# Layer 1 one-hot tables with token columns innermost, and constant bf16 ramps

## The chip, the cores and the metric

One core of a Trainium2 chip runs the whole program. The metric is the device time of one execution in microseconds (us), the median of a few runs.

## The reference, cut to what matters

Sixteen images and texts pass through a tokenizer, a selective-scan layer and a mixture of experts (layer 0), then through causal attention and a second mixture of experts (layer 1). Only the routing of the second mixture is touched:

```
logits = xf @ wr + br                      # tokens x 4 experts
topk_vals, topk_idx = top_k(logits, 2)     # each token has two experts
gates = softmax(topk_vals)
out = sum over the two of gates * (y_expert - c_expert + c_sum)
```

The 16 * 165 tokens are held as 22 tiles of up to 128 rows (16 text tiles, 6 image tiles), so there are 44 (choice, tile) columns.

## The kernel before, in words

**Tables of places.** The kernel sorts the (token, choice) pairs by expert into 48 slots (`SLOT1`) of 128 places. `positions` (line 571), on VectorE, works out for each pair its place; `high7` is the slot, `low7` the row in it. To invert that map it builds one-hot tables in bf16 and lets TensorE multiply them (lines 613 to 625):

- `intile1[p, i, 2, s]` is 1 where pair column i of token row p lies in slot s (line 616, 44 x 48 elements); `intile1[.., 0, ..]` is that times the tile number (line 619), `intile1[.., 1, ..]` that times the token row (line 621).
- `inrow1[p, i, r]` is 1 where the pair's row is r (line 624, in two halves of 22 columns i, 22 x 128 elements each).

The compares take one fp32 operand with the pair's number repeated along the inner dimension, and one fp32 constant (`k_slot`, `k_iota`) that runs along it; the product of line 619 reads the fp32 constant `k_tile`. So the innermost dimension is the slot (48) or the row (128), and each table is dense along it.

`pe_slots` (line 526) then runs 44 matmuls on TensorE into one PSUM bank: for column i the stationary operand is `inrow[:, i, :]` (128 dense columns) and the moving operand is `intile[:, i, :, :]` (3 x 48 = 144 dense columns). It waits for the first half of `inrow1` before column 0 and for the second before column 22. The matmul in the trace stands at line L531. The sum in PSUM holds, for each place, the tile, the row and whether it is taken; VectorE turns it into the lists `source` and `dest` (lines 637 to 645) by which GpSimd gathers and scatters rows.

**Order around it.** Engines run their instructions in the order written. On TensorE `pe_layer1` (line 1624) issues `biases_out(2)`, `pe_count`, `biases_sum` (line 1639: 96 matmuls at L1648 and 4 fp32 ones, recorded as 8, at L1651), the slot matmuls, and then the expert matmuls. On VectorE `positions` is followed by the last bias term (line 1703), two absolute maxima over weights (L658), the scale of the activations, and the experts. Layer 0 uses the same `positions` with one choice, 22 columns and 24 slots.

**Start of attention.** Layer 0's last expert output is scattered by GpSimd (L871) onto rows in DRAM; SyncE waits for that and loads the sums back as the residual `h`. ScalarE (`act_attention`, line 1321) meanwhile copies prepared weights (lines 1359 to 1363) and then takes the square roots for the first norm (`roots`, line 1364; the activation is at L1814). VectorE (`dve_attention`, line 1435) zeroes three small tiles, splits a bias (lines 1507 and 1508), waits for the last output product of layer 0 (`y_done`, line 1509) and for the first residual tiles (line 1510), and takes their statistics (L1439).

The buffer `X` holds layer 0's weights first, then the working tiles of attention (`rx`), then those of layer 1's experts (`rg`) in the same words. `early` holds the one-hot tables.

Of the kernel before, what the change touches and what calls it, by code (L numbers as in the profile page):

```python
# [8 lines left out]
BF16 = mybir.dt.bfloat16  # L9
# [3 lines left out]
ALU = mybir.AluOpType  # L13
ACT = mybir.ActivationFunctionType
# [3 lines left out]
P = 128  # L18
# [13 lines left out]
NT = BATCH + IT  # L32
# [7 lines left out]
SLOT0 = (BATCH * SEQ + G0 * (P - 1)) // P  # L40
W0N = 2 * KC * F0 + (F0 // P) * D

E1, F1, TOPK = 4, 1024, 2
T1 = 2 * P
PAIRS1 = (TOPK * BATCH * SEQ + E1 * (T1 - 1)) // T1
SLOT1 = 2 * PAIRS1
# [99 lines left out]
def known(i, value):  # L146

    return isinstance(i, int) and i == value
# [18 lines left out]
def build(nc, txt, patches, wtok, cols, rows_a, consts, pe_table, wsmall, w0, wattn, rows_f, w1, wsmall1,  # L167
          b2rows, out):
    with ExitStack() as ctx:
        def sb(name, shape, dt=F32):  # L170
            return ctx.enter_context(nc.sbuf_tensor(name, shape, dt))

        def sem(name):
            return ctx.enter_context(nc.semaphore(name))
# [4 lines left out]
        X = sb("X", [P, XW])  # L179
# [28 lines left out]
        low7 = rc[:, 0:TOPK, :].bitcast(I32)  # L208
        high7 = rc[:, TOPK:2 * TOPK, :].bitcast(I32)
# [3 lines left out]
        PS = ctx.enter_context(nc.psum_tensor("PS", [P, 8, 512], F32))  # L213
# [14 lines left out]
        k_slot = cst[:, at:at + SLOT1]; at += SLOT1  # L228
        k_far = cst[:, at:at + NT]; at += NT
        k_tile = cst[:, at:at + TOPK * NT]; at += TOPK * NT  # L230
        k_iota = cst[:, at:at + P]; at += P
        k_row, k_patch, k_class = (cst[:, at + i:at + i + 1] for i in range(3))
# [70 lines left out]
        XE = XW - W1W // 2 - 2 * E1 * D  # L303
# [4 lines left out]
        rx = Region(X, XE)  # L308
# [12 lines left out]
        oTi = rx.take([KC, PB * IMG])  # L321
        nmax, smax, psum_, rsum = (rx.take([2]) for _ in range(4))

        rg = Region(X, XE)
        early = Region(X, XE, rg.at)
        inrow1, intile1 = early.take([TOPK * NT, P], BF16), early.take([TOPK * NT, 3, SLOT1], BF16)
        hh1 = rg.take([2, 4, T1])
        wall1 = rg.take([SLOT1])
        bias1 = rg.take([2, F1 // P])
# [91 lines left out]
        y_done = sem("y_done")  # L421
        y_copied = sem("y_copied")
        y_out = [sem("y_out0"), sem("y_out1")]
        hot_ready = sem("hot_ready")
        map_psum = sem("map_psum")
# [92 lines left out]
        def pe_count(pe, done):  # L518
# [4 lines left out]
            nc.tensor.matmul(PS[:, 7, 128:128 + 4 * NT], onesb[:, :], flat, start=True, stop=True)\  # L523
                .then_inc(count_psum, 1)

        def pe_slots(pe, done, n, tiles, inrow, intile):

            for i in range(n):
                if i % (n // 2) == 0:
                    pe.wait_ge(hot_ready, 2 * done + i // (n // 2) + 1)  # L530
                ins = nc.tensor.matmul(PS[:, 7, 0:3 * tiles], inrow[:, i, :], intile[:, i, :, :].rearrange("p a b -> p (a b)"),  # L531
                                       start=(i == 0), stop=(i == n - 1))
            ins.then_inc(map_psum, 1)
# [30 lines left out]
        def dest_of_token(dve, chain, tiles, from_, to, taken):  # L564
# [3 lines left out]
            chain.link(nc.vector.tensor_tensor(to, spare[:, 0:tiles], to, ALU.subtract))  # L568
            chain.link(nc.vector.tensor_tensor(to, to, from_, ALU.add))

        def positions(dve, chain, choices, tiles, done, inrow, intile, unit):


# [9 lines left out]
            flat = lambda ap: ap.rearrange("p g t -> p (g t)")  # L583
# [17 lines left out]
            for c in range(choices):  # L601
# [4 lines left out]
            slots_of = posf[:, 0:choices, :]  # L606
# [3 lines left out]
            chain.link(nc.vector.tensor_scalar(high7[:, 0:choices, :], pos[:, 0:choices, :], 7, None,  # L610
                                               ALU.logical_shift_right))
            n = choices * NT
            chain.link(nc.vector.tensor_copy(slots_of, high7[:, 0:choices, :]))
            each = lambda ap, m: ap.rearrange("p c t -> p (c t)").unsqueeze(2).broadcast_to([P, n, m])
            along = lambda ap, m: ap.unsqueeze(1).broadcast_to([P, n, m])
            chain.link(nc.vector.tensor_tensor(intile[:, :, 2, :], each(slots_of, tiles), along(k_slot[:, 0:tiles], tiles),
                                               ALU.is_equal))
            chain.link(nc.vector.tensor_copy(slots_of, low7[:, 0:choices, :]))
            nc.vector.tensor_tensor(intile[:, :, 0, :], intile[:, :, 2, :],
                                    k_tile[:, 0:n].unsqueeze(2).broadcast_to([P, n, tiles]), ALU.mult)  # L620
            nc.vector.tensor_scalar(intile[:, :, 1, :], intile[:, :, 2, :], k_row, None, ALU.mult)
            half = n // 2
            for c0 in (0, half):
                nc.vector.tensor_tensor(inrow[:, c0:c0 + half, :], each(slots_of, P)[:, c0:c0 + half],
                                        along(k_iota, P)[:, c0:c0 + half], ALU.is_equal).then_inc(hot_ready, 1)

            units = tiles // unit
            sf = tok[:, 0, 0:units]
# [692 lines left out]
        def act_attention(act, roots):  # L1321
            act.wait_ge(small1_loaded, 16)
            nc.scalar.activation(gb1, c_b1c, ACT.Gelu).then_inc(gb_ready, 1)

            def image(n):
                act.wait_ge(xi_tr, n + 1)
                nc.scalar.activation(xTi[:, :, n * IROWS:(n + 1) * IROWS],
                                     PS[:, IMAGE_BANK[n], 0:KC * P].rearrange("p (k r) -> p k r", k=KC)[:, :, 0:IROWS],
                                     ACT.Copy).then_inc(xTi_copied, 1)

            def text(b, slot):
                act.wait_ge(xn_tr, AHEAD + NF + b + 1)
                nc.scalar.activation(xTb[:, slot, :, IMG:SEQ], PS[:, 7, 0:KC * P].rearrange("p (k r) -> p k r", k=KC),
                                     ACT.Copy).then_inc(xTb_copied, 1)

            def exps(b):
                act.wait_ge(s_max, b + 1)
                nc.scalar.activation(pA, sA1, ACT.Exp, bias=nmax[:, 0:1], scale=SCALE, accum_out=psum_[:, 0:1])
                nc.scalar.activation(pB[0:SEQ - P, :], sB1[0:SEQ - P, :], ACT.Exp, bias=nmax[0:SEQ - P, 1:2], scale=SCALE,
                                     accum_out=psum_[0:SEQ - P, 1:2]).then_inc(p_exp, 1)  # L1340

            def copy_pt(b):
                act.wait_ge(pt_psum, b + 1)
                nc.scalar.activation(pT1, PS[:, 4, 0:SEQ], ACT.Copy)
                nc.scalar.activation(pT2[0:SEQ - P, :], PS[0:SEQ - P, 4, SEQ:2 * SEQ - P], ACT.Copy).then_inc(pt_copied, 1)

            def copy_ot(b):
                act.wait_ge(ot_psum, b + 1)
                o_ = PS[:, 5, 0:KC * SEQ].rearrange("p (k r) -> p k r", k=KC)
                nc.scalar.activation(oTb, o_[:, :, IMG:SEQ], ACT.Copy).then_inc(ot_copied, 1)  # L1350
                nc.scalar.activation(oTi[:, :, bass.ds(b * IMG, IMG)], o_[:, :, 0:IMG], ACT.Copy).then_inc(ot_copied, 1)

            def chunk(n, k, j):

                act.wait_ge(stage_full[k], 16 * (j + 1))
                nc.scalar.activation(w1h[:, bass.ds(n * CW, CW)], stage[:, k, :], ACT.Copy).then_inc(w_high, 1)

            act.wait_ge(prep_psum, 3)
            nc.scalar.activation(wfT.rearrange("p k n -> p (k n)"), PS[:, 3, 0:KC * D], ACT.Copy)
            nc.scalar.activation(bfT, PS[:, 5, 0:KC], ACT.Copy).then_inc(prep_copied, 1)  # L1360
            act.wait_ge(prep_psum, 4)
            nc.scalar.activation(wfx[:, :, D:PAY1], PS[:, 5, 8:8 + KC * E1].rearrange("p (k e) -> p k e", k=KC), ACT.Copy)
            nc.scalar.activation(sums1, PS[:, 5, 8 + KC * E1:8 + (KC + 2) * E1], ACT.Copy).then_inc(prep_copied, 1)
            roots(0, BATCH + 1)
            image(0)
            text(0, 0)
            text(1, 1)
            roots(BATCH + 1, IT - 1)
            for n in range(1, IT):
                image(n)  # L1370


            def run(b, slot, j):
                exps(b)
                copy_pt(b)
                if known(b, 1):
                    roots(4, BATCH - 4)
                if not (isinstance(b, int) and b >= BATCH - 2):
                    text(b + 2, slot)
                copy_ot(b)  # L1380
                chunk(b, slot, j)
            run(0, 0, 0)
            run(1, 1, 0)
            with act.Fori(1, BATCH // 2 - 1) as j:
                run(2 * j, 0, j)
                run(2 * j + 1, 1, j)
            run(BATCH - 2, 0, BATCH // 2 - 1)
            run(BATCH - 1, 1, BATCH // 2 - 1)
# [46 lines left out]
        def dve_attention(dve, chain, inverse_roots):  # L1435
# [67 lines left out]
            chain.link(nc.vector.memset(smax[:, :], 0.0))  # L1503
            chain.link(nc.vector.memset(psum_[:, :], 1.0))
            chain.link(nc.vector.memset(raw1, 0.0))
            dve.wait_ge(gb_ready, 1)
            chain.link(nc.vector.tensor_copy(gbh, gb1))
            nc.vector.tensor_tensor(gbl, gb1, gbh, ALU.subtract).then_inc(gb_split, 1)
# [67 lines left out]
            for t in range(BATCH):  # L1576
                ins = nc.vector.bn_aggr(mv[:, t, :], stats[:, t, 0, :])
# [46 lines left out]
        def pe_layer1(pe):  # L1624
# [32 lines left out]
            biases_out(2)  # L1657
            pe_count(pe, 1)
            biases_sum()
            pe_slots(pe, 1, TOPK * NT, SLOT1, inrow1, intile1)  # L1660
            pe.wait_ge(slots_ready, 2)
            pe.wait_ge(dest_ready, 2)
            pe.wait_ge(rest_ready, 1)
# [775 lines left out]
```

## Time and profile before

| what | value |
|---|---|
| runs | 890.33 us median of 3 (890.0 to 891.31) |
| the profiled execution, its own time | 891.11 us |
| its span, first to last instruction | 889.3 us |
| granted TensorE clock, mean share of full speed | 0.935 |
| TensorE matmul busy | 776.2 us (87%), 5506 instructions |
| VectorE busy | 521.9 us (59%) |
| ScalarE busy | 366.0 us (41%) |
| GpSimd busy | 366.2 us (41%) |
| chain that ended last: TensorE, VectorE, GpSimd | 75%, 12%, 5% |

The profiled execution lies 0.78 us above the median. Its time is its span and 1.8 us around it. In the rows further down PE is TensorE's matmul, PEld its weight load, DVE VectorE, ACT ScalarE, POOL GpSimd, SPq the queue of SyncE; L531 is line 531 of the kernel, which can be that of a helper. A clock of 1.00 is TensorE's 2.4 GHz, 0.50 is 1.2 GHz.

### The profile page before, as it was taken

How to read it: one execution, taken by the hardware profiler on the slowest of the kernel's cores; microseconds unless marked ns; L12 is line 12 of the kernel's file. 1: busy time of each engine (PE TensorE's matmuls, PEld its weight loads, DVE VectorE, ACT ScalarE, POOL GpSimd, SP SyncE). 2: the span in 40 equal slices, each digit the busy share in tenths (PEclk: the TensorE clock that was granted, in tenths of full speed). 3: DMA queues.
4: the chain of work that ended last, by engine and by line, in shares of the span. 5: the costliest groups of instructions: out<-in, count | busy, mean ns of one | idle time of the engine just before them, and what ended most of it. 6: DMA issues, size and time to landing. Idle time of an engine off the chain costs nothing.

```text
span 889.3 us, 17678 instructions
## 1 busy us (share of the span) xinstructions
PE 776.2 (87%) x5506; PEld 609.1 (68%) x5507; DVE 521.9 (59%) x1300; ACT 366.0 (41%) x795; POOL 366.2 (41%) x314
## 2 busy tenths in 40 slices
PE   3898904999999999478999998958999999999991
PEld 2677802666666666356777776747898999999981
DVE  5898888433333333286777877884555555555550
ACT  5795671333333333224343343503444444444430
POOL 3349931223232322134455552012555555555442
PEclk9998965999999999878999997977999999999996
DMA  9950132232121111331111211521233332232325
GB/s 259 417 200 1 66 123 91 68 76 30 30 30 30 30 30 25 95 118 46 50 47 51 67 47 47 182 76 38 43 51 51 48 48 48 48 48 48 42 25 145
DMA packets 37042, 66.98 MB, mean 75 GB/s; under 512 B 3552, under 2 KB 29264, under 8 KB 35312
## 3 DMA queue, kind: packets, MB, share of 16 engines
q1 hardware_dynamic: 22992, 47.16, 15.9%
q0 software_dynamic: 13824, 19.01, 13.7%
q8 instruction: 19, 0.31, 0.2%
q10 hardware_dynamic: 192, 0.38, 0.1%
q14 instruction: 15, 0.12, 0.0%
HBM read 45.49 MB, written 23.74 MB: 78 GB/s over the span
## 4 chain that ended last, share of the span: by engine, by line
PE 75%; DVE 12%; POOL 5%; ACT 2%; DMA 2%; issue 1%; SPq 0%; POOLq 0%; DVEq 0%; ACTq 0%
PE PS L899 14%; PE PS L707 14%; PE PS L912 14%; PE PS L725 7%; PE PS L1208 5%; POOL X L1794 4%; PE PS L1218 3%; PE PS L1227 2%; PE PS L715 2%; PE PS L1256 2%; PE PS L1246 1%; PE PS L885 1%; DMA Y<-in_wtok_dram 1%; PE PS L1248 1%; PE PS L1969 1%
## 5 line engine op out<-in xcount | busy, mean ns | idle before, releaser
L1051 POOL DMA_INDIRECT sum<-X,dest x48 | 97.4, 2029 | 107.4 <-ACT X L966 95.3
L707 PE MATMUL PS<-X,Y 128*128 x576 | 134.3, 384 | 1.3 <-DVE Y L805 1.3
L912 PE MATMUL PS<-X 128*128 x768 | 133.5, 273 | 1.8 <-ACT X L966 1.8
L899 PE MATMUL PS<-X 128*128 128x256 f16 x768 | 130.2, 275 | 1.5 <-DVE X L984 1.5
L956 ACT ACTIVATE X<-PS,X 128x256 f32<-128x256 f32 x192 | 75.3, 475 | 109.9 <-PE PS L899 109.9
L899 PE MATMUL PS<-X,Y 128*128 128x256 f16 x384 | 105.5, 275 | 0.0
L912 PE MATMUL PS<-Y,X 128*128 x384 | 104.7, 273 | 0.0
L816 DVE SCALAR_TENSOR_TENSOR Y<-PS,Y 128x512 f32<-128x512 f32 x48 | 36.1, 751 | 111.5 <-PE PS L707 111.5
L871 POOL DMA_INDIRECT sum<-Y,dest x24 | 38.1, 1586 | 148.0 <-ACT Y L782 148.0
L707 PEld LDWEIGHTS PS<-X,Y 128*128 128x128 f16 x576 | 56.9, 99 | 60.8 <-issue 4.3
L899 PEld LDWEIGHTS PS<-X 128*128 x768 | 75.6, 99 | 11.4 <-issue 2.1
L912 PEld LDWEIGHTS PS<-X 128*128 128x128 f16 x768 | 75.1, 98 | 10.5 <-issue 2.1
L1038 POOL DMA_INDIRECT X<-xs,source x48 | 47.3, 985 | 70.5 <-DVE source L642 41.8
L725 PE MATMUL PS<-X,Y 128*128 x576 | 70.8, 273 | 2.4 <-DVE Y L822 1.7
L1011 DVE SCALAR_TENSOR_TENSOR PS<-PS,hscale,X 128x256 f32<-128x256 f32 x48 | 21.2, 488 | 79.1 <-PE PS L912 79.1
L1003 DVE SCALAR_TENSOR_TENSOR X<-X,hscale 128x1024 f16<-128x1024 f32 x48 | 61.6, 1284 | 1.7
L725 PEld LDWEIGHTS PS<-X,Y 128*128 128x128 f16 x576 | 56.1, 98 | 9.1 <-issue 3.1
L1794 POOL TENSOR_TENSOR X<-X 128x256 f16<-128x256 f32 (+1 forms) x55 | 58.2, 1097 | 0.5
L775 ACT ACTIVATE Y<-PS,hscale 128x512 f16<-128x512 f32 x48 | 33.0, 688 | 55.7 <-PE PS L715 55.7
L769 ACT ACTIVATE Y<-PS 128x512 f32<-128x512 f32 x48 | 28.7, 597 | 62.9 <-PE PS L707 62.9
L1405 POOL TENSOR_TENSOR X<-X 128x330 f32<-128x330 f32 x32 | 28.4, 886 | 62.7 <-DVE X L1467 62.7
L1208 PE MATMUL PS<-X,Y 128*128 128x165 f32 x256 | 47.0, 329 | 0.0
(356 smaller groups left out, 1499.1 us busy)
## 6 DMA issues: line engine op xcount, KB each, us to landing
X<-in_w_dram SPq DMA_DIRECT2D x11, 1024.0 KB, 17.4
stage<-in_w_dram SPq DMA_DIRECT2D x16, 512.0 KB, 3.5
sum<-h SPq DMA_DIRECT2D x2, 2048.0 KB, 7.5
xs<-Y SPq DMA_DIRECT2D x2, 1040.0 KB, 5.0
xs<-Y SPq DMA_DIRECT2D x2, 1032.0 KB, 5.5
h<-in_txt_dram SPq DMA_DIRECT2D x2, 1024.0 KB, 18.3
Y<-in_patches_dram SPq DMA_DIRECT2D x3, 672.0 KB, 8.8
sum<-h SPq DMA_DIRECT2D x2, 768.0 KB, 3.9
```

Source lines behind the costliest of these rows:

```text
L707: ins = nc.tensor.matmul(PS[:, 2 * u + s, 0:F0], x_[:, slot, k, :], w_[:, at_:at_ + F0], start=(n == 0), stop=(n == 3 * KC - 1))
L725: ins = nc.tensor.matmul(PS[:, 6, 0:D], h_[:, s, c, :], w_[:, at_:at_ + D], start=(s == 0 and c == 0 and n == 0), stop=(s == 1 and c == 3 ...
L816: nc.vector.scalar_tensor_tensor(out=hh[:, s, :].unsqueeze(1), in0=PS[:, 2 + s, 0:F0].unsqueeze(1), scalar=wall[:, bass.ds(i, 1), s], in1= ...
L871: nc.gpsimd.indirect_dma_start(out=sum0, out_offset=bass.IndirectOffsetOnAxis(ap=dest[:, i:i + 1], axis=0), in_=ybuf[:, i % 2, :], in_offs ...
L899: ins = nc.tensor.matmul(PS[:, 2 * s + c // 2, (c % 2) * T1:(c % 2 + 1) * T1], part[:, off:off + P], x_[:, slot, k, :], start=(n == 0), st ...
L912: ins = nc.tensor.matmul(PS[:, 4 + a, 0:D], h_[:, s, c, a * P:(a + 1) * P], part[:, off:off + D], start=(s == 0 and c == 0 and n == 0), st ...
L956: ins = nc.scalar.activation(hh1[:, s, c, :], PS[:, 2 * s + c // 2, (c % 2) * T1:(c % 2 + 1) * T1], ACT.Gelu, bias=bias1[:, slot, f:f + 1])
L1003: nc.vector.scalar_tensor_tensor(out=lo_, in0=act_, scalar=hscale[:, 2:3], in1=hi_, op0=ALU.mult, op1=ALU.subtract).then_inc(h1_lo, 1)
L1038: nc.gpsimd.indirect_dma_start(out=x1in[:, n // 2 % 2, n % 2, :], out_offset=None, in_=xs1, in_offset=bass.IndirectOffsetOnAxis(ap=source[ ...
L1051: nc.gpsimd.indirect_dma_start(out=sum1, out_offset=bass.IndirectOffsetOnAxis(ap=dest[:, i:i + 1], axis=0), in_=y1buf[:, i // 2 % 2, i % 2 ...
L1208: ins = nc.tensor.matmul(PS[:, bank, m * SEQ:(m + 1) * SEQ], w_[:, k, m * P:(m + 1) * P], xTb[:, slot, k, :], start=(k == 0), stop=(k == K ...
L1794: ins = nc.gpsimd.tensor_tensor(w0_low(n)[:, of], w0_landing(n)[:, of], w0_high(n)[:, of], ALU.subtract)
```

## The change

The tables of layer 1 are turned round: `inrow1` becomes [row, column] and `intile1` [kind, slot, column], with the 44 columns innermost. The operand that ran along the inner dimension becomes a filled table in bf16: `ramp_row` (128 x 44) and `ramp_tile` (44) are written by ScalarE ahead of `roots`, `ramp_slot` (48 x 44) by VectorE after a wait for `y_done`. They take 3,938 words of `X` behind attention's tiles. The pair's numbers are copied to bf16 (`lowb`, `highb`) and repeated along the middle dimension. TensorE now reads both operands with a step of 44 elements. Layer 0 keeps its form, in a function of its own (`one_hots0`).

```diff
@@ regions
+        ramp_row, ramp_slot = rx.take([P, TOPK * NT], BF16), rx.take([SLOT1, TOPK * NT], BF16)
+        ramp_tile = rx.take([TOPK * NT], BF16)
+        lowb, highb = rx.take([TOPK * NT], BF16), rx.take([TOPK * NT], BF16)
...
-        inrow1, intile1 = early.take([TOPK * NT, P], BF16), early.take([TOPK * NT, 3, SLOT1], BF16)
+        inrow1, intile1 = early.take([P, TOPK * NT], BF16), early.take([3, SLOT1, TOPK * NT], BF16)
@@ TensorE
+        def pe_slots1(pe):
+
+            n = TOPK * NT
+            for i in range(n):
+                if i % NT == 0:
+                    pe.wait_ge(hot_ready, 2 + i // NT + 1)
+                ins = nc.tensor.matmul(PS[:, 7, 0:3 * SLOT1], inrow1[:, :, i],
+                                       intile1[:, :, :, i].rearrange("p a b -> p (a b)"), start=(i == 0), stop=(i == n - 1))
+            ins.then_inc(map_psum, 1)
@@ VectorE, for layer 1 in place of lines 613 to 625
+        def one_hots1(chain):
+
+            n = TOPK * NT
+            each = lambda ap, m, k: ap.unsqueeze(1).broadcast_to([P, m, k])
+            flat = lambda ap: ap.rearrange("p c t -> p (c t)")
+            nc.vector.tensor_copy(highb, flat(high7))
+            chain.link(nc.vector.tensor_copy(lowb, flat(low7)))
+            chain.link(nc.vector.tensor_tensor(intile1[:, 2], each(highb, SLOT1, n), ramp_slot, ALU.is_equal))
+            nc.vector.tensor_tensor(intile1[:, 0], intile1[:, 2], each(ramp_tile, SLOT1, n), ALU.mult)
+            nc.vector.tensor_scalar(intile1[:, 1], intile1[:, 2], k_row, None, ALU.mult)
+            for c0 in (0, NT):
+                of = slice(c0, c0 + NT)
+                nc.vector.tensor_tensor(inrow1[:, :, of], each(lowb[:, of], P, NT), ramp_row[:, :, of], ALU.is_equal)\
+                    .then_inc(hot_ready, 1)
@@ ScalarE, in act_attention ahead of roots(0, BATCH + 1)
+            spread = lambda ap, n: ap.unsqueeze(2).broadcast_to([P, n, TOPK * NT])
+            nc.scalar.activation(ramp_row, spread(k_iota, P), ACT.Copy)
+            nc.scalar.activation(ramp_tile, k_tile, ACT.Copy)
@@ VectorE, in dve_attention behind the memsets (ahead of line 1506)
+            dve.wait_ge(y_done, SLOT0)
+            nc.vector.tensor_copy(ramp_slot, k_slot.unsqueeze(2).broadcast_to([P, SLOT1, TOPK * NT]))
@@ pe_layer1
-            pe_slots(pe, 1, TOPK * NT, SLOT1, inrow1, intile1)
+            pe_slots1(pe)
```

## Rows read from the trace of the kernel before

**Rows 1.** The page: the chain that ended last, by line.

```profile
PE PS L899 14%; PE PS L707 14%; PE PS L912 14%; PE PS L725 7%; PE PS L1208 5%; POOL X L1794 4%; PE PS L1218 3%; PE PS L1227 2%; PE PS L715 2%; PE PS L1256 2%; PE PS L1246 1%; PE PS L885 1%; DMA Y<-in_wtok_dram 1%; PE PS L1248 1%; PE PS L1969 1%
```

**Rows 2.** The chain in order of time, 578 to 606 us: start us, us, what.

```profile
578.98 2.37 DVE X L616
...
584.63 6.01 DVE X L624 x2
...
590.69 2.83 PE PS L531 x22
...
593.55 0.22 DVE stats L637
...
602.03 0.77 PE PS L683 x2
```

**Rows 3.** VectorE's groups with shapes kept apart: mean ns after the busy time.

```profile
L624 DVE TENSOR_TENSOR X<-posf,cst 128x2816 bf16<-128x2816 f32 x2 | 6.1, 3084 | 0.0
...
L624 DVE TENSOR_TENSOR Y<-posf,cst 128x1408 bf16<-128x1408 f32 x2 | 3.2, 1618 | 0.0
...
L619 DVE TENSOR_TENSOR X<-X,cst 128x2112 bf16<-128x2112 bf16 x1 | 2.4, 2357 | 0.0
...
L621 DVE TENSOR_SCALAR X<-X,cst 128x2112 bf16<-128x2112 bf16 x1 | 0.8, 762 | 0.0
```

**Rows 4.** TensorE's timeline around 584 to 591 us.

```profile
583.92 1.99 PE L1651 MATMUL PS<-X,onesf 1*128 1x256 f32 x8
587.69 1.94 PE L531 MATMUL PS<-X 128*128 128x144 bf16 x22 [1.78 <-DVE X L624]
```

**Rows 5.** TensorE's slot matmuls and weight loads, line L531.

```profile
L531 PEld LDWEIGHTS PS<-X x44: 95/151/152, 587.7 to 593.1; 128*128 128x128 bf16 x44
L531 PE MATMUL PS<-X x44: 226/327/328, 587.7 to 593.2; 128*128 128x144 bf16 x44
```

**Rows 6.** Short stretches around the slot matmuls: PE, PEld, DVE, ACT, POOL, clock, DMA.

```profile
587.60:588.20 0.60, 0.51 (x8) 0.51 (x9) 0.60 (x2) 0.00 (x0) 0.00 (x0) 1.00 0.00 0
...
588.80:589.40 0.60, 0.60 (x8) 0.54 (x5) 0.60 (x1) 0.00 (x0) 0.00 (x0) 0.50 0.00 0
```

**Rows 7.** VectorE's reductions, by shape (L553 reads at a step of 22 words).

```profile
L1484 DVE TENSOR_REDUCE X<-X 128x1 f32<-128x128 f32 x16 | 4.6, 286 | 0.6
...
L553 DVE TENSOR_REDUCE ra<-ra 128x22 f32<-128x88 f32 x2 | 0.6, 301 | 0.1
...
L593 DVE TENSOR_REDUCE sm<-ra 128x4 f32<-128x44 f32 x1 | 0.2, 199 | 0.0
```

**Rows 8.** ScalarE's timeline before attention, and its later square root.

```profile
371.04 1.28 ACT L1814 ACT_TABLE_LOAD   x1
378.45 0.22 ACT L1814 ACTIVATE rs<-rs 128x17 f32<-128x17 f32 x1 [6.13 <-DVE rs L2140]
```

**Rows 9.** ScalarE's copies and exponentials by shape.

```profile
L1356 ACT ACTIVATE X<-stage 128x1024 f16<-128x1024 f32 x4 | 4.2, 1058 | 0.0
...
L1338 ACT ACTIVATE X<-X 128x128 f32<-128x128 f32 x16 | 6.4, 402 | 29.9 <-DVE X L1485 29.9
```

**Rows 10.** VectorE's timeline while the residual is awaited.

```profile
368.11 0.18 DVE L1507 CAST wsm<-wsm 128x32 f16<-128x32 f32 x1 [3.50 <-ACT wsm L1323]
...
376.00 1.73 DVE L1439 BATCH_NORM_STATS2 stats<-h 128x6 f32<-128x256 f32 x5 [7.47 <-DMA h<-sum]
```

**Rows 11.** The chain in order of time, 355 to 382 us.

```profile
364.39 1.58 PE PS L725 x12
...
366.75 3.82 DMA sum<-Y,dest
```

**Rows 12.** GpSimd's scatters: line L871, and one of L1051 in the timeline.

```profile
L871 POOL DMA_INDIRECT sum<-Y,dest x24: 1552/1587/1624, 166.0 to 366.7; - x24
...
648.01 2.34 POOL L1051 DMA_INDIRECT sum<-X,dest  x1 [3.83 <-ACT X L966]
```

**Rows 13.** VectorE's timeline beside that scatter.

```profile
647.60 1.28 DVE L1003 SCALAR_TENSOR_TENSOR X<-X,hscale 128x1024 f16<-128x1024 f32 x1
```

More of the change, by code:

```diff
@@ L322, in build @@
         nmax, smax, psum_, rsum = (rx.take([2]) for _ in range(4))
-        rg = Region(X, XE)
-        early = Region(X, XE, rg.at)
-        inrow1, intile1 = early.take([TOPK * NT, P], BF16), early.take([TOPK * NT, 3, SLOT1], BF16)
+        ramp_row, ramp_slot = rx.take([P, TOPK * NT], BF16), rx.take([SLOT1, TOPK * NT], BF16)
+        ramp_tile = rx.take([TOPK * NT], BF16)
+        lowb, highb = rx.take([TOPK * NT], BF16), rx.take([TOPK * NT], BF16)
+        ramps_at = rx.at - TOPK * NT * (P + SLOT1 + 3) // 2
+        rg = Region(X, ramps_at)
+        early = Region(X, ramps_at, rg.at)
+        inrow1, intile1 = early.take([P, TOPK * NT], BF16), early.take([3, SLOT1, TOPK * NT], BF16)
         hh1 = rg.take([2, 4, T1])
@@ L569, in dest_of_token, with one_hots0 @@
             chain.link(nc.vector.tensor_tensor(to, to, from_, ALU.add))
+        def one_hots0(chain, slots_of, inrow, intile):
+            chain.link(nc.vector.tensor_copy(slots_of, high7[:, 0:1, :]))
+            each = lambda ap, m: ap.rearrange("p c t -> p (c t)").unsqueeze(2).broadcast_to([P, NT, m])
+            along = lambda ap, m: ap.unsqueeze(1).broadcast_to([P, NT, m])
+            chain.link(nc.vector.tensor_tensor(intile[:, :, 2, :], each(slots_of, SLOT0), along(k_slot[:, 0:SLOT0], SLOT0),
+                                               ALU.is_equal))
+            chain.link(nc.vector.tensor_copy(slots_of, low7[:, 0:1, :]))
+            nc.vector.tensor_tensor(intile[:, :, 0, :], intile[:, :, 2, :],
+                                    k_tile[:, 0:NT].unsqueeze(2).broadcast_to([P, NT, SLOT0]), ALU.mult)
+            nc.vector.tensor_scalar(intile[:, :, 1, :], intile[:, :, 2, :], k_row, None, ALU.mult)
+            half = NT // 2
+            for c0 in (0, half):
+                nc.vector.tensor_tensor(inrow[:, c0:c0 + half, :], each(slots_of, P)[:, c0:c0 + half],
+                                        along(k_iota, P)[:, c0:c0 + half], ALU.is_equal).then_inc(hot_ready, 1)
+        def one_hots1(chain):
[11 more added lines that the diff above has]
+                    .then_inc(hot_ready, 1)
         def positions(dve, chain, choices, tiles, done, inrow, intile, unit):
@@ L612, in positions @@
             n = choices * NT
[L613 to L625, printed above, removed]
+            if choices == 1:
+                one_hots0(chain, slots_of, inrow, intile)
+            else:
+                one_hots1(chain)
             units = tiles // unit
```

## The prediction

> **What bounds the kernel now.** The page is read first: the chain that ended last belongs mostly to TensorE's expert products, and no line of this change is in its list [rows 1]. So the share of busy time says nothing here; the chain in order of time does. From 578.98 us it runs through VectorE's one-hot tables of layer 1 (L616 to L624, until 590.64 us), then through the last 22 slot matmuls until 593.52 us, and at 593.55 us VectorE reads the result [rows 2]. Behind that come small chained steps, two maxima over weights and, at 602.03 us, TensorE's first work for the experts [rows 2]. Between the slot matmuls and that point VectorE is never without work and TensorE has none, so whatever moves 593.52 us moves the end by as much. The reader should see two candidates for that point: VectorE's tables, and TensorE, whose timeline shows it busy with the bias sums until 585.91 us and idle for only 1.78 us before the first slot matmul [rows 4].
>
> **The tables on VectorE.** Five large instructions are replaced by five with the same numbers of elements. Now each two-source one takes one element per cycle or so: 1,408 elements take 1,618 ns, 2,816 take 3,084 and 2,112 take 2,357 [rows 3]. No row shows a two-source instruction whose operands are all 2-byte. Its bounds are no gain (2,357 and 3,084 ns) and the rate of the one-source instruction that is all bf16, 2,112 elements in 762 ns [rows 3]. I take the middle, two elements per cycle: a half of `inrow1` then costs what 1,408 elements cost now, 1.62 us, and a table of 2,112 some 1.26 us (the fixed part is 2 * 1,618 - 3,084 = 152 ns, the rest halves). The scalar product stays at 0.76 us, its rate being reached already. The two small copies stand where two stood. Counted from 578.98 us, allowing 0.1 us for the copy that now comes earlier: 579.1, plus 1.26, 1.2 and 0.7, then 1.55 for a half (successive ones overlap a little). The first half is ready at about 583.9 us in place of 587.69, the second at 585.4 in place of 590.64. That is 5.2 us of VectorE time gone.
>
> **What is late next.** TensorE does the bias sums first, in program order, and their last fp32 products could be followed at 585.75 us at the earliest: 1.99 us for 8, each lasting 0.387 us, gives a pitch of 0.23 us, and the next one starts a pitch after the eighth [rows 4]. So the faster tables are worth 1.94 us at the first half, and from there all 44 matmuls run without a wait. Their end is 585.75 us + 43 pitches + 0.35 us of the last one's own time and its semaphore. It was 593.52 us, so the break-even pitch is 173 ns.
>
> **The pitch of a slot matmul.** Now it is 8 starts in 0.51 us, 63 ns, while the clock is 1.00, and at 0.50 it is (2.83 - 0.327) / 21 = 119 ns [rows 2, 5, 6]: 144 columns at one per cycle of 2.4 or 1.2 GHz. The weight loads take 95 to 152 ns and run beside the matmuls [rows 5]. Afterwards every column of both operands is 88 bytes from the last. No row shows TensorE reading so. The lower bound is no cost, 63 ns. The nearest row for the other end is VectorE's reduction at L553, which reads fp32 at this very step of 22 words: contiguous reductions take 286 ns for 128 elements and 199 ns for 44, so 1.036 ns each and 153 ns fixed, which makes 245 ns for 88; L553 takes 301 [rows 7]. That is 0.64 ns more per element, 1.68 ns in all. If this is the time in which the memory gives one element of a distant line, it holds for TensorE too whatever its clock, and 144 columns take 242 ns. I take 242 ns, since it is the only row with this step; the end is then 585.75 + 43 * 0.242 + 0.35 = 596.5 us, which is 3.0 us late.
>
> The page "SBUF — State Buffer" of the Trainium skill (section Door 1, its note on cachelines) speaks against this change: the memory has lines of 16 bytes, at least two accesses must fall in one to hide its latency, and 8 bf16 elements is as far as a step goes free. The row of L553 agrees in kind. The page gives no price for TensorE; without the rule the sum would be that of the first rival below. "VectorE: DVE Perf Modes" (The perf-mode tier table) gives two elements per cycle for an all-bf16 two-source instruction; no row here shows it.
>
> **The ramps on ScalarE.** One copy of 5,632 elements and one of 44. A copy of 1,024 takes 1,058 ns and an exponential of 128 takes 402 [rows 9], so 0.73 ns per element and 4.5 us at the least, 5.8 us if everything scales with 1,058; with the small one 4.7 to 6.0 us. The queue is free when the table load of 1.28 us begins, at 371.04 us; the load then comes behind the copies, and the square root is wanted at 378.45 us [rows 8]: it would be ready between 377.0 and 378.3 us. The cover is the wait for the residual; it costs nothing, with 0.15 us left at the slow end. Behind these copies stand only the roots, for which VectorE waits.
>
> **The ramp on VectorE.** 2,112 elements, between 0.76 [rows 3] and 2.36 us. VectorE is idle until 368.11 us and again from 368.5 to 376.00 us [rows 10], and its wait for `y_done` ends with layer 0's last product at 365.97 us [rows 11], so itself it delays only the bias split, which TensorE first uses for layer 1's bias sums, after the whole of attention. But it lies beside GpSimd's last scatter, issued at 366.75 us, which is on the chain too [rows 11]. The scatters of layer 0 take 1,587 ns; one that begins at 648.01 us, beside VectorE's two-input product until 648.88 us, takes 2,340 [rows 12, 13]. So 0.87 us side by side costs 0.75 us. A copy at two elements per cycle would run from 366.05 to 367.35 us, 0.6 us beside the scatter: plus 0.5 us. Bounds: nothing, and 1.4 us for a copy of 2.36 us.
>
> **Sum.** 3.0 + 0.5 = 3.5 us. The sum is against the profiled execution (891.11 us, so 894.6 us); against the median of the runs, 0.78 us lower, it is 890.33 + 3.5 = **893.8 us**. No DMA is added or moved, and SyncE's queue is passed by nothing. A measurement of this kernel can tell about 0.2%, 1.8 us, from no change.
>
> **The rivals.**
> - Distant columns are free for TensorE. It starts warm at 585.75 us, straight behind the bias sums, and the clock, which fell to 0.50 here after the 1.78 us gap [rows 4, 6], need not fall. 585.75 + 43 * 0.063 + 0.25 = 588.7 us, 4.8 us early; with the scatter 4.3: 886.0 us. This is the other side; it decides below 173 ns of pitch. For it: no row shows TensorE itself losing anything to a step. Against: L553. Chance 0.24.
> - Half speed, 120 ns: 585.75 + 5.16 + 0.3 = 591.2 us, 2.3 early, with the scatter 1.8 us: 888.5 us, at the edge of what can be told. For it: a penalty in cycles of the reader's own clock (L553 loses 0.6 of a cycle per element). Chance 0.19, and 0.05 for pitches around the break-even.
> - The weight loads, 128 distant columns, 215 ns by the same row, no longer run beside the matmuls: pitch 457 ns, end 605.8 us, 12.2 late: 903 us. Against it: they overlap now [rows 5]. Chance 0.05.
> - The change doesn't do what it says: the all-bf16 compares stay at one element per cycle. The first half is then ready at 587.7 us as now, and with 242 ns the end is 598.5 us: 5.5 us in all, 895.8 us (0.04); with plain pitches, nothing moves (0.01).
> - Likeliest, 893.8 us: 0.42.
>
> **The numbers.** Slower: 0.42 + 0.05 + 0.04 = 0.51. The half-speed case is split, 0.12 to no change and 0.07 to faster; with 0.05 and 0.01 no change has 0.18. Faster: 0.24 + 0.07 = 0.31. Cases of both signs hold much of the chance, so the range reaches from 885.6 (columns free, a scatter undisturbed) to 896.5 us (the compares at one per cycle, the scatter at its bound) and leaves out the serial weight loads and tails. The likeliest case's own range is 892.3 to 895.6 us.
>
> **What would show it.** Right: bf16 tables of 1.26 and 1.62 us; slot matmuls from 585.8 us on in one run of 44 without a gap, at a pitch near 0.24 us; a longer last scatter at L871 in attention's start, and the first statistics about 0.5 us later; the square root still waiting for VectorE. Wrong: a pitch of 63 or 120 ns, or a clock that falls amid them and changes the pitch, which would say that it is counted in TensorE's cycles and not in the memory's time.

## The result, and the profile after

The changed kernel takes 897.29 us (median of 6), the kernel before 890.82 us in the same comparison: a ratio of 1.0076, interval 1.0055 to 1.0097, so 4.9 to 8.6 us slower. One of the six runs of the kernel before took 4,457.89 us; it moves the median little, and the ratio is taken from the undisturbed runs. The forecast said slower, 893.8 us, and the range ended at 896.5 us. The sign and most of the steps held; one term was sized too small.

The chain of the changed kernel in order of time, 575 to 608 us (start us, us, what), beside [rows 2]:

```profile
574.99 7.64 PE PS L1690 x70
582.63 1.92 PE PS L1693 x8
584.55 14.81 PE PS L537 x44
...
599.39 0.22 DVE stats L674
...
602.66 4.40 DVE tops L695 x2
...
607.86 0.77 PE PS L720 x2
```

VectorE's tables are no longer in it. TensorE's bias sums (L1690, L1693) are followed at once by all 44 slot matmuls (L537), which take 14.81 us. The stretch from the first copy of the pair's numbers to VectorE's read of the result lasts from 577.39 to 599.39 us, 22.0 us; before it was 14.79 us (578.76, the copy just ahead of L616's 578.98, to 593.55 [rows 2]). That is 7.2 us lost in one place. The profiled span grew by only 5.5 us (894.8 against 889.3), because this execution was already 1.5 us ahead at layer 0's first scatter (164.5 against 166.0 us [rows 12]), where nothing is changed. Behind VectorE's read the two run alike: 295.4 us to the end, against 295.7 before.

VectorE's timeline of the changed kernel, 575 to 600 us:

```profile
577.39 0.19 DVE L607 CAST X<-rc 128x44 bf16<-128x44 int32 x1
...
577.70 1.26 DVE L609 TENSOR_TENSOR X<-X 128x2112 bf16<-128x2112 bf16 x1
579.00 1.26 DVE L610 TENSOR_TENSOR X<-X 128x2112 bf16<-128x2112 bf16 x1
580.17 0.76 DVE L611 TENSOR_SCALAR X<-X,cst 128x2112 bf16<-128x2112 bf16 x1
580.85 3.15 DVE L614 TENSOR_TENSOR X<-X 128x2816 bf16<-128x2816 bf16 x2
...
599.39 0.21 DVE L674 COPY stats<-PS 128x48 f32<-128x48 f32 x1 [14.46 <-PE PS L537]
```

The tables cost 1.26, 1.26, 0.76 and 3.15 us, as against 2.37, 2.36, 0.76 and 6.1 us [rows 2, 3]. Then VectorE waits 14.46 us for TensorE. The reader should see the trade: 5 us less on one engine, some 10 us more on the one behind it (its 44 matmuls took 1.94 and 2.83 us before [rows 2, 4]).

Line L537 of the changed kernel (duration ns min/median/max), beside [rows 5]:

```profile
L537 PEld LDWEIGHTS PS<-X x44: 153/156/177, 584.5 to 598.5; 128*128 128x128 bf16 x44
L537 PE MATMUL PS<-X x44: 523/524/529, 584.5 to 598.8; 128*128 128x144 bf16 x44
```

And short stretches of it. Each line has its length and the busy time of TensorE, its weight load, VectorE, ScalarE and GpSimd, then the granted clock (1.00 or 0.50 here) and, last, two figures on DMA:

```profile
584.50:586.00 1.50, 1.50 (x6) 0.83 (x6) 0.39 (x2) 0.39 (x1) 0.00 (x0) 1.00 0.00 0
...
588.00:590.00 2.00, 2.00 (x8) 0.93 (x6) 0.00 (x0) 0.00 (x0) 0.00 (x0) 0.50 0.00 0
```

A matmul starts every 333 ns, at 1.00 as at 0.50: 44 of them in 14.81 us, and those that start before the clock falls at 587.3 us have the same pitch as those behind.

ScalarE and GpSimd at the start of attention (timeline of ScalarE; then the scatter's line):

```profile
369.22 4.90 ACT L1402 ACTIVATE X<-cst 128x5632 bf16<-128x5632 f32 x1
...
374.25 1.28 ACT L1856 ACT_TABLE_LOAD   x1
377.01 0.22 ACT L1856 ACTIVATE rs<-rs 128x17 f32<-128x17 f32 x1 [1.48 <-DVE rs L2182]
```

```profile
L908 POOL DMA_INDIRECT sum<-Y,dest x24: 1552/1588/2006, 164.5 to 365.2; - x24
```

The ramps cost ScalarE 5.1 us and are hidden with 1.48 us to spare. The last scatter, beside VectorE's copy into `ramp_slot`, takes 2.01 us in place of 1.55. Little of that arrives further on. From this scatter's start to landing it is 4.21 us against 3.82, but the load of the residual behind it took 4.62 us against 4.91, so the first statistics follow the scatter's start by 9.35 us (365.20 to 374.55), against 9.25 before (366.75 to 376.00).

### The profile page after: what moved, and what is told of

The parts are those of the page before. It is cut to its first block, busy times and chain, and to the rows that moved or that the text cites. A ratio compares the mean times of both kernels' runs of the same rounds, so it can differ in the third digit from the quotient of the medians.

```text
span 894.8 us, 17681 instructions
## 1 busy us (share of the span) xinstructions
PE 785.3 (88%) x5506; PEld 611.2 (68%) x5507; DVE 517.2 (58%) x1301; ACT 370.5 (41%) x797; POOL 365.5 (41%) x314
## 4 chain that ended last, share of the span: by engine, by line
PE 78%; DVE 10%; POOL 5%; ACT 2%; DMA 2%; issue 1%; SPq 0%; POOLq 0%; DVEq 0%; ACTq 0%
PE PS L936 14%; PE PS L744 14%; PE PS L949 14%; PE PS L762 7%; PE PS L1245 5%; POOL X L1836 4%; PE PS L1255 3%; PE PS L1264 2%; PE PS L752 2%; PE PS L1293 2%; PE PS L537 2%; PE PS L1283 1%; PE PS L922 1%; PE PS L1285 1%; DMA Y<-in_wtok_dram 1%
```

## The experiments

What stayed open was what 333 ns is made of. Theory A: the moving operand's distant columns alone, 2.3 ns each. Theory B: the two operands' readings one after the other, 156 ns for the stationary one (the weight load's time above) and the rest, 178 ns, for the moving one. In what follows an operand is called turned when it is read with a step of 44 elements, and dense when its columns are adjacent.

**Probes between the tables and the slot matmuls.** The changed kernel with extra matmuls into an unused PSUM bank; their results are not used.

```diff
+        def pe_probes(pe):
+            pe.wait_ge(hot_ready, 4)
+            row_ = ramp_row.rearrange("p a b -> p (a b)")
+            turned = lambda i: intile1[:, :, :, i].rearrange("p a b -> p (a b)")
+            mm = lambda to_, left, right: nc.tensor.matmul(to_, left, right, start=True, stop=True)
+            for i in range(16):
+                mm(PS[:, 3, 0:144], onesb[:, :], turned(i))
+            for i in range(16):
+                mm(PS[:, 3, 0:144], inrow1[:, :, i], row_[:, 0:144])
+            for i in range(16):
+                mm(PS[:, 3, 0:144], onesb[:, :], row_[:, 0:144])
+            for i in range(16):
+                mm(PS[:, 3, 0:48], inrow1[:, :, i], turned(i)[:, 0:48])
...
```

> The turned kernel with 256 extra matmuls between the tables and the slot matmuls (16 groups of 16, one source line each, results unused), dense and with column steps of 2 to 44 elements, on the moving or the stationary side. Theory A: the pitch of 334 ns is the moving operand's reading alone, 144 distant columns at 2.3 ns each. Then a dense stationary with the turned moving operand has 334 ns, and a turned stationary with a dense moving operand stays near 63 to 156 ns. Theory B: the two operands' readings don't run beside each other, 156 ns for the stationary and 178 ns for the moving columns. Then each alone has about 156 to 180 ns. Both: steps of 2 and 4 elements (4 and 8 bytes) cost nothing, 63 ns warm; from 8 elements (16 bytes) on the pitch is that of 44. With 48 turned moving columns A gives about 110 ns or the load's 156, B about 215 ns.

TensorE's timeline of this kernel (the groups share one line, so they are told apart by time and by the tiles that they read; `onesb` is the dense stationary operand):

```profile
585.14 5.49 PE L535 MATMUL PS<-X,onesb 128*128 128x144 bf16 x16
590.44 2.11 PE L535 MATMUL PS<-X 128*128 128x144 bf16 x16
592.35 2.12 PE L535 MATMUL PS<-X,onesb 128*128 128x144 bf16 x16
...
619.46 6.50 PE L535 MATMUL PS<-X 128*128 128x144 bf16 x80
```

and its clock around the last three of them:

```profile
590.50:592.30 1.80, 1.80 (x17) 1.80 (x16) 0.00 (x0) 0.00 (x0) 0.00 (x0) 0.50 0.00 0
592.40:594.20 1.80, 1.80 (x18) 1.80 (x16) 0.00 (x0) 0.00 (x0) 0.00 (x0) 0.50 0.00 0
...
622.00:625.00 3.00, 3.00 (x49) 3.00 (x48) 0.00 (x0) 0.00 (x0) 0.00 (x0) 0.99 0.02 5
```

Dense stationary with turned moving operand: 5.30 us from group to group, 331 ns each. Turned stationary with dense moving operand: 1.91 us, 119 ns, and the group with both dense that follows has the same at the same clock of 0.50. The last 80 have a dense moving operand and stationary steps of 2, 4, 8, 16 and 32 elements: 120 ns each up to 622 us, at 0.50, and at a clock of 0.99 some 47 of them start in 3.0 us, 64 ns each. Theory A holds: the moving side pays it all, and what the stationary side does stays hidden beside it. With only 48 turned moving columns the pitch is 113 ns, where A had expected about 110 or the load's 156, and B 215. The time of this kernel is 938.3 us, the probes included.

In one point both theories were wrong: a step of 4 was to be free and one of 8 or more was to cost what 44 does. Six groups with a dense stationary operand follow, with moving steps of 2, 4, 8, 16, 32 and 1 elements; the windows lie in the groups of 8 and of 32:

```profile
601.40 18.26 PE L535 MATMUL PS<-X,onesb 128*128 128x144 bf16 x96
...
605.40:608.30 2.90, 2.90 (x14) 1.37 (x12) 0.00 (x0) 0.00 (x0) 0.00 (x0) 1.00 0.00 0
...
613.70:617.50 3.80, 3.80 (x17) 1.95 (x16) 0.00 (x0) 0.00 (x0) 0.00 (x0) 0.50 0.00 0
```

From start to start the groups of 8, 16 and 32 have 256, 261 and 244 ns, not 333; at 0.50 the group of 4 has 130 ns, where the group of 2 has 119 and dense ones 120. So the price of a step had to be measured by itself (below).

**One operand turned at a time, in the kernel itself.** `moving_only` keeps `inrow1` dense, `stationary_only` keeps `intile1` dense.

```diff
# moving_only
-        inrow1, intile1 = early.take([P, TOPK * NT], BF16), ...
+        inrow1, intile1 = early.take([TOPK * NT, P], BF16), ...
-                nc.vector.tensor_tensor(inrow1[:, :, of], each(lowb[:, of], P, NT), ramp_row[:, :, of], ALU.is_equal)\
+                nc.vector.tensor_tensor(inrow1[:, of], lowb[:, of].unsqueeze(2).broadcast_to([P, NT, P]),
+                                        k_iota.unsqueeze(1).broadcast_to([P, NT, P]), ALU.is_equal)\
...
# stationary_only
-early.take([3, SLOT1, TOPK * NT], BF16)
+early.take([TOPK * NT, 3, SLOT1], BF16)
...
```

> As the turned kernel, but inrow1 stays dense (its compare at one element per cycle, 3.08 us a half) and only the moving operand intile1 is turned. Theory A: the slot matmuls keep their pitch of 334 ns, and their end is the turned kernel's plus about 1.5 us at most for the later first half. Theory B: the pitch falls to about 178 ns, and the slots end some 5 us earlier than in the turned kernel.

> Only inrow1 is turned (a step of 44 on the stationary side), intile1 stays dense with its compare and product at one element per cycle (2.36 us each). Theory A, that only the moving side pays for its step: the slot matmuls run at 63 to 65 ns when warm and end some 4 us earlier than in the kernel before: about 886 us. Theory B, that the sides add up: a pitch of 220 ns or more, and about 893 us.

The chain of `moving_only`, then that of `stationary_only`:

```profile
583.27 1.92 PE PS L1694 x8
585.19 14.77 PE PS L537 x44
```

```profile
581.41 2.36 DVE X L612
583.77 0.68 DVE X L613
584.45 1.55 DVE X L616
586.04 3.25 PE PS L537 x44
589.31 0.22 DVE stats L676
```

With only the moving operand turned the 44 matmuls take 14.77 us, all of the loss (897.31 us in one run). With only the stationary one turned they take 3.25 us (its weight loads take 151 ns each, beside the matmuls), the kernel's stretch is 10.6 us (578.70 to 589.31) in place of 14.8, and it is faster than the kernel before: 885.69 against 890.49 us, ratio 0.9959, interval 0.9936 to 0.9981. So half of the change was a gain of about 4 us, and the other half lost it and 7 us more.

**The size of the step.** `pad48` pads the table rows to 48 columns; `probes2` puts 23 groups of 10 dense-stationary matmuls with moving steps of 1 to 64 elements ahead of the slots, results unused.

```diff
# pad48
+        inrow1, intile1 = early.take([P, 48], BF16), early.take([3, SLOT1, 48], BF16)
+        inrow1, intile1 = inrow1[:, :, 0:TOPK * NT], intile1[:, :, :, 0:TOPK * NT]
# probes2, one group, here a step of 4
+            for i in range(10):
+                nc.tensor.matmul(PS[:, 3, 0:144], onesb[:, :], flat16[:, 0:576:4], start=True, stop=True)
```

> The turned kernel with its table rows padded from 44 to 48 columns, so a step of 96 bytes in place of 88. Theory L: a column costs 1.7 to 1.8 ns where its step is a multiple of the 16-byte line and 2.3 ns where it is not. Then the pitch falls from 333 to about 250 ns, and the slots end 3.6 us earlier. Theory D: the cost grows with the distance. Then the pitch is 333 ns or more.

> The turned kernel with 23 groups of 10 extra matmuls ahead of the slots, a dense stationary operand, and 144 moving columns with steps of 1 to 8, 12, 16, 20, 22, 24, 28, 32, 36, 40, 44, 46, 48, 52 and 64 elements of 2 bytes, results unused. Theory L: about 250 ns at 8, 16, 24, 32, 40, 48 and 64; about 333 ns at 12, 20, 22, 28, 36, 44, 46 and 52. Theory D: a rise with the step. Both: 1 and 2 at 63 or 119 ns by the clock, 4 at 130 ns.

Padding made it worse. Its chain has

```profile
588.20 15.97 PE PS L538 x44
```

that is a pitch of 360 ns, from the first start at 588.13 to the last at 603.60 us (902.4 us in one run). The groups of `probes2` (953.4 us in one run, the extra matmuls included) have a line each; steps of 1, 2, 3, 4 and 8 elements, then 32, 36, 40, 44, 48, 52 and 64 (the groups left out are in the tables below):

```profile
587.89 0.80 PE L535 MATMUL PS<-X,onesb 128*128 128x144 bf16 x10
588.53 0.80 PE L537 MATMUL PS<-X,onesb 128*128 128x144 bf16 x10
589.17 1.14 PE L539 MATMUL PS<-X,onesb 128*128 128x144 bf16 x10
590.15 1.46 PE L541 MATMUL PS<-X,onesb 128*128 128x144 bf16 x10
...
597.22 2.74 PE L549 MATMUL PS<-X,onesb 128*128 128x144 bf16 x10
...
615.03 2.62 PE L563 MATMUL PS<-X,onesb 128*128 128x144 bf16 x10
617.47 2.91 PE L565 MATMUL PS<-X,onesb 128*128 128x144 bf16 x10
620.20 3.18 PE L567 MATMUL PS<-X,onesb 128*128 128x144 bf16 x10
623.20 3.52 PE L569 MATMUL PS<-X,onesb 128*128 128x144 bf16 x10
...
629.99 3.79 PE L573 MATMUL PS<-X,onesb 128*128 128x144 bf16 x10
633.59 2.93 PE L575 MATMUL PS<-X,onesb 128*128 128x144 bf16 x10
636.34 2.62 PE L577 MATMUL PS<-X,onesb 128*128 128x144 bf16 x10
```

From the start of one group to that of the next, through ten matmuls, the pitch is as follows. The granted clock was 1.00 up to the step of 6, fell within the group of 7, and was 0.50 from 8 on:

| step, elements of 2 bytes | 1 | 2 | 3 | 4 | 5 | 6 | 7 | 8 |
|---|---|---|---|---|---|---|---|---|
| ns for 144 columns | 64 | 64 | 98 | 128 | 161 | 193 | 225 | 256 |

| step | 12 | 16 | 20 | 22 | 24 | 28 | 32 | 36 | 40 | 44 | 46 | 48 | 52 | 64 |
|---|---|---|---|---|---|---|---|---|---|---|---|---|---|---|
| ns | 253 | 261 | 256 | 255 | 252 | 248 | 244 | 273 | 300 | 332 | 347 | 360 | 275 | 244 |

Both theories on the step fall. L (multiples of the line against others) gave 12, 20, 22 and 28 the high price, and they have the low one; 48 was to be low and is the highest. D (a rise with the distance) is right only up to 8 and from 32 to 48. Three regions are shown: from 4 to 16 bytes the pitch is 32 ns times the step; from 16 to 64 bytes it is flat, 244 to 261 ns or 1.7 to 1.8 ns per column; around 96 bytes stands a peak of 2.50 ns per column, gone at 128 bytes. The change's 88 bytes lie on the slope of that peak. Both clocks were seen at 8 bytes (groups of 4, below), at 16 (`probes`), at 88 (the changed kernel) and at 96 (`pad48`), each time with the same pitch; the other steps above 16 bytes were measured at 0.50 alone. What makes the peak was not found. The section "5.2 Measured stream behaviour on trn2" of "Vector Engine (DVE) Microarchitecture Reference" in the Trainium skill has 2.50 to 2.51 ns per column for VectorE at a step of 24 words, the same 96 bytes and the same time as TensorE's at 48 elements here.

**Groups: a small step for TensorE, pairs for VectorE.** If VectorE's higher rate needs no more than two adjacent columns, the tables can be turned within groups of 2 or 4.

```diff
+        G = 2
+        GR = TOPK * NT // G
+        ramp_row, ramp_slot = rx.take([P, G], BF16), rx.take([SLOT1, G], BF16)
+        inrow1, intile1 = early.take([GR, P, G], BF16), early.take([GR, 3, SLOT1, G], BF16)
...
+                ins = nc.tensor.matmul(PS[:, 7, 0:3 * SLOT1], inrow1[:, i // G, :, i % G],
+                                       intile1[:, i // G, :, :, i % G].rearrange("p a b -> p (a b)"), ...
```

> The 44 columns in 22 groups of 2: inrow1 is [group, row, 2], intile1 [group, kind, slot, 2], so VectorE still has two adjacent columns innermost and TensorE a step of 2 elements. The ramps shrink to 256 and 96 elements. If VectorE's two-per-cycle rate needs only a pair, the tables stay at 1.26 and 1.62 us; if a step of 4 bytes is free for TensorE, the slot matmuls run straight behind the bias sums at 63 ns: 2.8 us in place of 14.8 us. The time would be 4.8 us under the kernel before, about 886 us. If the step costs as 44 does, it is the turned kernel's time, 897 us; if VectorE falls back to one per cycle, the kernel before's, 891 us.

> The same with 11 groups of 4: a step of 8 bytes for TensorE. Both theories expect what groups of 2 give, about 886 us, if two accesses in a line of 16 bytes are what it needs; if every step costs in proportion, a pitch between 63 and 334 ns and a time between 886 and 897 us.

The chain with groups of 2, then that with groups of 4:

```profile
582.11 1.92 PE PS L1695 x8
584.03 2.98 PE PS L539 x44
587.04 0.22 DVE stats L676
```

```profile
582.65 5.91 PE PS L539 x44
```

Groups of 2: the tables still take 1.26, 1.26 and 3.15 us, the slot matmuls start straight behind the bias sums at 65 ns each, and the time is 885.52 against 890.03 us, ratio 0.996, interval 0.9944 to 0.9976. The stretch fell from 14.79 to 10.18 us (576.86 to 587.04), 4.6 us. Groups of 4: 131 ns each, at 1.00 as at 0.50, and a stretch of 13.1 us. The ratio is 1.0001 (0.9982 to 1.002), so the 1.7 us that the stretch still gains can't be told in the times. A step of 8 bytes is not free: it gives back 2.9 of the 4.6 us, more than both theories allowed.

**What binds next.** With groups of 2 TensorE came to the slots 0.5 us behind VectorE's second half. The four fp32 products at the end of the bias sums were moved behind the slot matmuls.

```diff
             biases_sum()          # without the four matmuls on b2all
             pe_slots1(pe)
+            b2_sum()              # the four matmuls, into the same sum
```

> Groups of 2, and the four fp32 matmuls of the b2 rows (1.9 us) moved from the end of the bias sums to behind the slot matmuls, into TensorE's idle time while VectorE works. If TensorE's bias sums are what the slot matmuls wait for in the kernel with groups of 2 (they start 0.5 us behind the second table half there), the slots end at VectorE's second half plus 1.5 us, about 1.7 us earlier, and the time falls to about 884 us. If VectorE then waits for the sum (line of csum), up to 0.4 us of it is lost. If the bias sums did not matter, the time stays that of groups of 2.

Its chain from 578 us:

```profile
580.80 3.04 PE PS L539 x44
...
585.79 0.39 ACT X L1662
...
586.21 1.28 DVE X L1750 x2
587.49 4.40 DVE tops L697 x2
```

The stretch is 8.3 us (575.57 to 583.88), 1.9 us less than with groups of 2, and 0.25 us of it is lost again to the wait for ScalarE's copy of the sum. The time is 882.19 against 890.49 us, ratio 0.9919, interval 0.9892 to 0.9946: the version that beats both kernels. By the stretch its gain is 6.2 us; the median shows 8.3 with an interval from 4.8 to 9.6 us.

## Why the prediction was right or wrong

- **VectorE's tables: right.** Two elements per cycle were taken, 1.26 us for a table and 1.62 us for a half of `inrow1`; the profile has 1.26 us, and 3.15 us for the two halves together. The rival in which they stay at one per cycle fell. (The sum puts the first half at 583.9 us where its terms give 583.8; nothing hangs on it.)
- **TensorE becomes the bound, from the end of the bias sums: right.** The 44 matmuls ran without a gap behind them. The kernel with groups of 2 shows the same point of start with the cheap pitch, 4.6 us better, against 4.8 in the first rival's sum.
- **The pitch of a slot matmul: the step that failed.** The prediction said "I take 242 ns, since it is the only row with this step". It is 333 ns, and 43 pitches turn 3.0 us of loss into 6.9. Two things were wrong in it. L553 does not stream with that step: it reduces over four experts, so it makes three hops of 88 bytes and comes back to the next tile, whereas the moving operand makes 143 in a row. That this is why it costs less was not tried. And the 1.7 ns per column taken from it is a real price, but that of steps from 16 to 64 bytes; 88 bytes is dearer. The break-even of 173 ns was passed either way, which is why the sign was right; since the price came from another engine's short hops, the sign owes something to luck. The rivals of free columns (63 ns) and of half speed (120 ns) fell.
- **Not counted in TensorE's clock: right.** The clock fell amid the slot matmuls and the pitch stayed: 333 ns at 1.00 and at 0.50. That it is the memory which sets it is argued and not shown.
- **The stationary side is hidden: right.** In `stationary_only` the 44 take 3.25 us, against 2.98 us with groups of 2, though a weight load takes 151 ns there and 97 with groups of 2: at most 6 ns a matmul. The rival of serial weight loads fell.
- **The rule on lines** (the Trainium skill, "SBUF — State Buffer", Door 1) was the right warning, but its measure of 8 bf16 elements for free is not what these runs show: at a clock of 1.00 a step of 3 already costs 98 in place of 64 ns, and 8 costs 256 (`probes`, 605.4 to 608.3 us).
- **ScalarE's ramps: right,** 5.1 us against 4.7 to 6.0, hidden.
- **The scatter beside VectorE's copy: right in size, its effect on the end too large.** Plus 0.46 us against 0.5. In `stationary_only` and `pad48`, which also have that copy, the last scatter takes 2.00 and 2.01 us; with groups of 2, whose copy writes 96 elements, no scatter takes over 1,624 ns. But the first statistics came only 0.10 us later after it, where 0.5 was expected, since the load in between was 0.29 us shorter in this execution. In the runs here that load takes 4.3 to 4.9 us, so what the scatter costs in the end is not shown to better than a few tenths.
- **The sum.** 6.9 us, 0.2 for a last matmul of 524 ns and 0.1 for a slightly later start make the 7.2 us of the stretch; with 0.1 to 0.4 us from the scatter it is 7.3 to 7.6, inside the interval of 4.9 to 8.6. With 242 ns in it the sum was 3.5 us, below it. The upper end of the range was also 0.2 us low by its own terms, 4.9 + 1.4 us, or 896.7; the measured 897.29 us lies outside that too.

## What to carry to other kernels

Before turning a table round for VectorE, look at what TensorE will read as its moving operand: there a step of 2 bf16 elements was free and one of 3 not, while for the stationary operand steps of 2 to 44 cost 6 ns a matmul at most. For the compares and the product here VectorE's higher two-source rate needed only two adjacent 2-byte elements, so an interleave of 2 served both engines. And price a long stream by a long stream: a row whose inner loop is short is no measure of its step.

## What the runs showed of the hardware that was not expected

- TensorE's moving operand of 144 bf16 columns costs 32 ns per element of step from 2 to 8 elements, which is 1.78 ns for each 16 bytes passed over. At a step of 8 (`probes`) it is the same at both clocks; at steps of 1 and 2 the clock sets the pitch, 64 ns at 1.00 and 119 to 120 at 0.50.
- At a step of 96 bytes a column costs 2.50 ns, but at 32 to 64 and at 128 bytes 1.7 to 1.8.
- The granted clock fell from 1.00 to 0.50 at 587.3 us of the changed kernel (mean 0.82 from 586 to 588 us), although TensorE issued slot matmuls without a gap, one per 333 ns. With groups of 4, one per 131 ns and no gap either, it fell at 585.4 us, amid them. With groups of 2, where they come every 65 ns, it stayed at 1.00 through them. But all 44 last only 3.0 us there, and in the changed kernel the clock fell 2.8 us behind the first of them, so that the slow pitch is the cause is not shown. Groups of 2:

```profile
584.00:585.00 1.00, 1.00 (x17) 1.00 (x17) 0.35 (x2) 0.39 (x1) 0.00 (x0) 1.00 0.00 0
...
586.00:587.00 1.00, 1.00 (x16) 0.81 (x13) 0.00 (x0) 0.00 (x0) 0.00 (x0) 1.00 0.00 0
```
